# Bias sum over the second weight's rows: products on ScalarE and additions on GpSimd in place of VectorE's multiply-adds

## The reference

```python
x = x + (x @ W0.T + b0 + 2 * (x @ A0[idx0]) @ B0[idx0])
x = x + (x @ W1.T + b1 + (x @ A1[idx1].T) @ B1[idx1].T)
return x
```

## Time and profile before

| | us |
|---|---|
| median of 3 runs | 307.51 |
| lowest, highest | 307.34, 307.9 |
| the profiled execution | 307.65 |
| its span | 306.1 |
| TensorE busy | 300.6 |
| VectorE busy | 194.5 |
| ScalarE busy | 89.4 |
| GpSimd busy | 18.5 |

### The profile page before, as it was taken

One profiled execution on the slowest core, in us unless ns is written; L12 is line 12 of the kernel. 1 busy time (PEld: TensorE's weight loads), 2 busy tenths in 40 slices (PEclk: granted clock), 3 DMA queues, 4 the chain that ended last, 5 costly groups with the idle time before them and its releaser, 6 DMA issues.

```text
span 306.1 us, 4010 instructions
## 1 busy us (share of the span) xinstructions
PE 300.6 (98%) x1429; PEld 250.5 (82%) x1429; DVE 194.5 (64%) x327; ACT 89.4 (29%) x143; POOL 18.5 (6%) x43
## 2 busy tenths in 40 slices
PE   7999999999999999999999999999999999999995
PEld 6888898888887688888888888888888888888884
DVE  5777624894749450499998487486485585585312
ACT  4555534012023302392234232231321222231000
POOL 2433130000000010000000000000000000000000
PEclk9999999999999999999999999999999999999999
DMA  7996160000000055504161540641721611702002
GB/s 274 376 350 237 40 167 20 0 0 2 0 0 3 16 177 208 173 5 137 55 229 55 164 140 34 200 137 40 209 86 71 217 42 71 224 34 103 2 34 103
DMA packets 14745, 33.94 MB, mean 111 GB/s; under 512 B 2406, under 2 KB 2406, under 8 KB 14727
## 3 DMA queue, kind: packets, MB, share of 16 engines
q1 hardware_dynamic: 13702, 31.60, 30.2%
q0 software_dynamic: 1024, 2.10, 2.3%
HBM read 22.09 MB, written 11.60 MB: 110 GB/s over the span
## 4 chain that ended last, share of the span: by engine, by line
PE 97%; DVE 1%; ACT 1%; issue 0%
PE bank L800 29%; PE bank L912 17%; PE bank L911 17%; PE bank L913 17%; PE bank L931 5%; PE bank L812 3%; PE bank L918 2%; PE bank L828 2%; PE bank L889 1%; PE bank L887 1%; PE bank L888 1%; PE bank L814 1%; PE bank L860 1%; PE bank L898 1%; PE bank L884 1%; DVE stage L670 0%
## 5 line engine op out<-in xcount | busy, mean ns | idle before, releaser
L800 PE MATMUL bank<-w,w_hi 128*128 128x512 f32 x256 | 78.2, 390 | 0.0
L800 PEld LDWEIGHTS bank<-w,w_hi 128*128 128x128 f32 x256 | 47.9, 188 | 10.7 <-issue 0.9
L800 PE MATMUL bank<-w,w_lo 128*128 128x512 f32 x128 | 49.0, 389 | 0.0
L401 ACT CAST xa<-xr 128x512 fp32r<-128x512 f32 x32 | 19.6, 621 | 34.2 <-PE bank L918 15.7
L800 PEld LDWEIGHTS bank<-w,w_lo 128*128 128x128 f32 x128 | 24.0, 188 | 5.0
L912 PE MATMUL bank<-w_lo,w 128*128 128x512 f32 x64 | 25.1, 392 | 0.0
L913 PE MATMUL bank<-w_hi,w 128*128 128x512 f32 x64 | 25.1, 392 | 0.0
L911 PE MATMUL bank<-w_hi,w 128*128 128x512 f32 x64 | 25.0, 391 | 0.0
L912 PE MATMUL bank<-w 128*128 128x512 f32 x64 | 25.0, 391 | 0.0
L911 PE MATMUL bank<-w 128*128 128x512 f32 x64 | 25.0, 391 | 0.0
L911 PE MATMUL bank<-w_hi,xa 128*128 128x512 f32 x64 | 25.0, 390 | 0.0
(11 more groups left out here) (123 smaller groups left out, 502.7 us busy)
## 6 DMA issues: line engine op xcount, KB each, us to landing
xr<-xT SPq DMA_DIRECT2D x32, 256.0 KB, 4.3
out<-stage SPq DMA_DIRECT2D x28, 256.0 KB, 2.0
stage<-W SPq DMA_DIRECT2D x8, 512.0 KB, 5.1
stage<-W1T SPq DMA_DIRECT2D x8, 512.0 KB, 6.2
a<-rb_rows SPq DMA_DIRECT2D x8, 392.0 KB
rb_rows<-a SPq DMA_DIRECT2D x3, 512.0 KB
rb_rows<-b0w SPq DMA_DIRECT2D x3, 512.0 KB
out<-rows SPq DMA_DIRECT2D x4, 256.0 KB, 2.8
```

The costliest lines, as they stand in the source:

```text
L401: nc.scalar.copy(x_op(j, 0), raw(j)).then_inc(op_hi[j], 1)
L800: return mm(d_bank(m, h)[:, :], left[:, m, k * P:(k + 1) * P], right[:, k, h * HALF:(h + 1) * HALF], start=start, stop=stop)
```

## The change

VectorE's 16 operations go. ScalarE makes the products, 32 of 128x512, in the order high part left, high part right, low part left, low part right for each slice k, into three buffers `bias_part` (the last quarters of the three slots of `stage`), used in turn. GpSimd adds each to its half of `bias_sum`, also 32 operations. ScalarE's product n waits until addition n - 3 is done; GpSimd's addition n waits for product n and for addition n - 2, the last one on the same half. Semaphore `bias_step` now counts to 32. On ScalarE the products stand in four groups of eight, at places that answer to VectorE's former ones. On GpSimd the additions stand after the B1 loads and before the A0 loads. VectorE's `factors` gets a wait for `aux_done`.

```diff
--- before.py
+++ after.py
@@ -90,6 +90,9 @@
         b1_hl = b0w_flat[:, 0:2 * D].rearrange("p (s n) -> p s n", s=2)
         h_stack = [b0w_flat[:, s * T:(s + 1) * T] for s in range(2)]
         c_hl = [c_rows[32 * part:32 * part + B, :] for part in range(2)]
+
+
+        bias_part = [stage[:, n, 3 * HALF:4 * HALF] for n in range(3)]
 
 
         t_raw = {t: stage[:, n, :].rearrange("p (k n) -> p k n", k=KH) for n, t in enumerate((T2, T3, T4))}
@@ -167,6 +170,7 @@
         t_zeroed = sem("t_zeroed")
         t_bounced = sem("t_bounced")
         t_landed = sem("t_landed")
+        bias_scaled = sem("bias_scaled")
         bias_step = sem("bias_step")
         st_step = sem("st_step")
         r_summed = sem("r_summed")
@@ -330,6 +334,14 @@
                 i1 = adapter(B + b)
                 pool.dma_start(b1_raw[b * RK:(b + 1) * RK, :],
                                B1[bass.ds(i1, 1), :, :].rearrange("s r n -> (s r) n")).then_inc(b1_landed, DMA)
+            pool.wait_ge(bias1_landed, DMA)
+            for n in range(4 * KT):
+                cols = slice(n % 2 * HALF, (n % 2 + 1) * HALF)
+                pool.wait_ge(bias_scaled, n + 1)
+                if n >= 2:
+                    pool.wait_ge(bias_step, n - 1)
+                nc.gpsimd.tensor_tensor(bias_sum[:, cols], bias_sum[:, cols], bias_part[n % 3], ALU.add
+                                        ).then_inc(bias_step, 1)
             for b in range(2, B):
                 load_a0(b)
 
@@ -379,6 +391,13 @@
                 nc.scalar.copy(t_raw[T3][:, m, :], b[:, :]).then_inc(top_copied, 1)
                 act.wait_ge(top_t1, m + 1)
                 nc.scalar.copy(w0_hi[:, m, HALF:D], t_raw[T2][:, m, :]).then_inc(top_t1_hi, 1)
+
+            def bias_scale(k):
+                for n in range(4):
+                    part, cols = (w1_hi, w1_lo)[n // 2], slice(n % 2 * HALF, (n % 2 + 1) * HALF)
+                    if 4 * k + n >= 3:
+                        act.wait_ge(bias_step, 4 * k + n - 2)
+                    nc.scalar.mul(bias_part[(4 * k + n) % 3], part[:, k, cols], b0_raw[:, k:k + 1]).then_inc(bias_scaled, 1)
 
             def high_bottom(m):
                 wait_summed(m)
@@ -429,15 +448,23 @@
             aux_copy(4)
             high_bottom(4)
             high_top(1)
+            bias_scale(0)
+            bias_scale(1)
             high_bottom(5)
             aux_copy(5)
+            bias_scale(2)
+            bias_scale(3)
             high_top(2)
             aux_copy(6)
+            bias_scale(4)
+            bias_scale(5)
             high_bottom(6)
             aux_copy(7)
             aux_copy(8)
             for j in (A11, A21, A12, A22):
                 high_x(j, 0)
+            bias_scale(6)
+            bias_scale(7)
 
             for h in range(NH):
                 act.wait_ge(r_summed, h + 1)
@@ -552,15 +579,6 @@
                 nc.vector.tensor_tensor(t_raw[T4][:, t, :], c[:, :], t_raw[T2][:, t, :], ALU.subtract
                                         ).then_inc(t4_made, 1)
 
-            def bias_add(k):
-                for n, part in enumerate((w1_hi, w1_lo)):
-                    if 2 * k + n == 0:
-                        dve.wait_ge(bias1_landed, DMA)
-                    else:
-                        dve.wait_ge(bias_step, 2 * k + n)
-                    nc.vector.scalar_tensor_tensor(out=bias_sum, in0=part[:, k, :], scalar=b0_raw[:, k:k + 1],
-                                                   in1=bias_sum, op0=ALU.mult, op1=ALU.add).then_inc(bias_step, 1)
-
             def low_x(j, b):
                 dve.wait_ge(op_hi[j], b + 1)
                 nc.vector.tensor_tensor(x_op(j, 1), raw(j), x_op(j, 0), ALU.subtract).then_inc(op_lo[j], 1)
@@ -600,6 +618,7 @@
                 g = g_all[:, :, b * RK:(b + 1) * RK]
                 a0 = a0_raw[:, s, :].rearrange("p (k r) -> p k r", k=KT)
                 dve.wait_ge(a0_landed[s], (b // 2 + 1) * DMA)
+                dve.wait_ge(aux_done, len(AUX))
                 if b >= 2:
                     dve.wait_ge(h_summed, b - 1)
                 nc.vector.tensor_copy(to[:, :, 0:RK], a0).then_inc(aa_hi, 1)
@@ -693,21 +712,13 @@
             g_add(4)
             low_bottom(4)
             low_top(1)
-            bias_add(0)
-            bias_add(1)
             low_bottom(5)
             g_add(5)
-            bias_add(2)
-            bias_add(3)
             low_top(2)
             g_add(6)
-            bias_add(4)
-            bias_add(5)
             low_bottom(6)
             g_add(7)
             g_add(8)
-            bias_add(6)
-            bias_add(7)
             for j in (A11, A21, A12, A22):
                 low_x(j, 0)
 
@@ -891,7 +902,7 @@
 
             pe.wait_ge(d_lo[B11], 3)
             pe.wait_ge(top_t1, 3)
-            pe.wait_ge(bias_step, 2 * KT)
+            pe.wait_ge(bias_step, 4 * KT)
             for h in range(NH):
                 cols = slice(h * HALF, (h + 1) * HALF)
                 bank = d_bank("c", h)
```

## The result

The changed kernel takes 308.5 us in the median of 8 runs (308.24 to 308.99), against 307.58 for the kernel before beside it. The ratio is 1.0037, with a 95% interval of 1.0026 to 1.0048: slower by 0.8 to 1.5 us. The time lies in the range of the prediction, and of the three directions "slower" had been given the largest chance, 0.51. The forecast itself (a stall of 0.46 us, 308.0) is not what happened.

What follows compares the result with a forecast made beforehand. TensorE was taken to bound the kernel, busy 300.6 of 306.1 us. The profiled 307.65 plus a 0.46 us stall, all other terms 0, gave 308.1; less 0.14, 308.0 us. Range: 307.4 to 309.5.

Steps and rivals of the forecast that it cites:

- VectorE's relief is worth 0: VectorE: removing sixteen operations, 20.5 us beside full TensorE stretches, was costed at 0.
- ScalarE's products are covered: ScalarE: 32 products at 0.52 us, 16.6 us in all, fit idle gaps of 9.5 to 10.6 us.
- The groups' ends on ScalarE: ScalarE: last products of the four groups through at 63.8, 73.1, 84.5 and 100.7 us; later work late without cost.
- The place of the loss: TensorE's bias matmuls: they wait for GpSimd's last additions, 0.46 us, passed on whole.
- My own sign of being wrong: TensorE's bias matmuls: a wait of more than 1 us there would show the forecast wrong.
- the price *a* of an addition: GpSimd: each 128x512 addition costs 1.17 us, the middle between 0.86 and 1.49.
- 8*a* - 8.9: TensorE's bias matmuls: stall from eight last-group additions, sum seen at 94.28 + 8a against a start at 103.18; 0.46 us.
- the meeting: GpSimd's last group beside VectorE's low parts of x: a lock adds 0.3 us, giving 308.3; chance 0.15 alone.
- The case of the price: GpSimd's additions cost more, stall above 0.6 us from a = 1.19; most likely 308.6 us; chance 0.36.
- Faster: VectorE's earlier copies shorten some unseen wait of TensorE; 307.1 us; chance 0.05.
- the round trip of the rows: Transfers still leave at 104.63; TensorE's product at 126.89 keeps its time, a later TensorE only gains slack.
- my upper case: GpSimd additions at a = 1.49: ScalarE's groups run late, the last ends at 108.7, a stall of 5.6 us.

Runs made afterwards that it cites:

- the swap: The last eight ScalarE products placed ahead of the four x casts instead of behind them, against the changed kernel; 308.05 us, ratio 1.0032.

## Why the prediction was right, and where it was not

- *VectorE's relief is worth 0*: right, and shown by leaving the sum out (ratio 1.000). VectorE's busy time fell by 19.7 us (predicted 20.5). `low_x` did start early, at 91.48 (92.04 on the clock of before, predicted 92.0), and nobody gained.
- *ScalarE's products are covered*: right in the sum, off in the price. I took the x casts' 0.52 us; a product takes 0.72, not 0.62, and comes 0.61 behind the last. The casts have no factor; the product takes one for each partition from SBUF. The Trainium skill has this under "ScalarE: Activation LUTs", section "What ACT_TABLE_LOAD costs": a pointer operand adds about 93 ns, and the trace agrees with 0.1 us. I had the row of a cast and not that sentence. It moved the first addition by less than 0.1 us.
- *The groups' ends on ScalarE*: group 1 at 63.85, group 2 at 73.84, group 3 at 84.69 in the changed kernel; predicted, less 0.56: 63.2, 72.5, 83.9. `high_top(2)` started at 73.75, 0.3 us behind the time when it was due (74.01 less 0.56), and that was covered: TensorE's list has no wait there. The first r copy came at 100.78 (predicted 100.7 less 0.56, so 0.6 later), which nobody felt, and the rows left at 104.08 (104.63 less 0.55), as predicted.
- *The place of the loss*: right. TensorE waits at the bias matmuls for GpSimd, once. The path, the place and the fact that a wait is passed on were right; the amount was not. My own sign of being wrong, a wait of more than 1 us there, came true with 1.3, and so did, by 0.12 us, the sign of additions that stretch beside VectorE.
- *The size*: the term that was mis-sized is the price *a* of an addition, 1.17 us against a measured 1.25. Eight times 0.08 are 0.64 us, more than the whole stall of the forecast: in 8*a* - 8.9 a small error of *a* becomes a large one of the stall. To these 0.64 come 0.12 from the first addition meeting the last low part of x (1.42 us long, 1.30 for the others), and some 0.15 to 0.2 from the longer product, the last addition's own length and the hop to TensorE. From 0.46 that makes 1.4, and TensorE's row shows 104.00 - 102.63 = 1.37. That the time still fell into the range is owed to the width of the range, which had been set for this case too. I took the middle between two bounds scaled from 128-element selects, with a second operand in the upper one only, at the 0.83 ns an element of a memset; the true value lay in the upper half. (The lower bound's own sum is 4 x 0.20 + 0.04 = 0.84, not 0.86; the middle stays at 1.17.) An addition costs 2.15 ns an element in all. How much of this is the second operand no run separates.
- *The rivals*: both slower ones came true together, the price with most of the weight and the meeting with 0.12 us where I had given it 0.3. The case of the price had 308.6 us; measured were 308.5. Faster and "paced by ScalarE" did not occur: within a group GpSimd's additions follow each other without a gap.
- *What the prediction overlooked*: that a second edge lies close. I wrote that the round trip of the rows "stands" and gains slack when TensorE is late. True here, since the wait at L909 hid it; but without that wait 0.1 to 0.2 us is all there is, which the swap ran into. And my upper case, a stall of 5.6 us for *a* = 1.49, left out the clock: waits of 3.5 and 3.7 us were each followed by a time at half the granted clock, so a wait of 5.6 would probably have cost more than its length. No run has that case.

The version without a loss (products ahead of the x casts, low parts of x behind the c rows) reaches the kernel before and doesn't beat it; TensorE has no hole that the bias sum could fill. The first 8 us, where executions differ by half a microsecond, were not studied.

## What to carry to other kernels

Work taken from an engine that nobody waited for gained nothing here, while the engine that received it made a new wait: compare the end of its last burst, the count times its own price, with the moment when the result is wanted. Price a two-operand GpSimd operation by its own measurement: here a length of 0.18 us plus 2.15 ns an element. At 512 elements its starts lie 1.25 us apart, twice the 0.60 of VectorE. Where a wait is removed, look for the next edge before expecting its time back: here the rows' round trip had 0.1 to 0.2 us of slack.

## What the runs showed of the hardware that I had not expected

- VectorE loses more than GpSimd when both read two SBUF operands: 557 to 1344 ns for its 128x384 addition, against 1.25 to 1.56 us from start to start for GpSimd's 128x512. Moving one VectorE operand to PSUM took both losses away.
- Making a TensorE wait 2.4 us longer, 3.7 us in place of 1.3, cost 4.8 us, through half the granted clock behind it. Before the wait of 1.3 us and after it the granted clock was full, and it cost its own length.
